# Narrow score products, and expert results weighted in the tile and added by DMA into the output

## The reference, cut to what matters

```python
# layer 0: shifted windows of 64 tokens, 8 heads of 8 channels
qn, kn = q / |q|, k / |k|
attn = einsum('whnd,whmd->whnm', qn, kn) * scale + bias[idx] + mask
out = einsum('whnm,whmd->whnd', softmax(attn), v) @ Wo.T + bo
...
# last layer: 8 experts of width 682, the two best of each token
probs = softmax(flat @ router_w.T)
top_p, top_i = top_k(probs, 2);  top_p = top_p / (sum(top_p) + 1e-9)
h = silu(w1[e] @ x) * (w3[e] @ x);  y[e] = w2[e] @ h
out[n] = t[n] + sum over the two e of top_p * y[e][n]      # t: the residual
```

## Time and profile before

| | |
|---|---|
| median of 3 runs | 1230.27 us (1229.73 to 1235.08) |
| the profiled execution | 1225.98 us, its span 1224.1 us |
| TensorE busy | 957.1 us (78%) |
| VectorE, ScalarE, POOL busy | 814.1, 697.4, 645.7 us |
| moved by DMA | 39.37 MB |

### The profile page before, as it was taken

The page is one execution under the profiler, slowest core; times in us unless marked ns, Lnnn a source line. Parts: engine busy times, 40 slices in busy tenths (PEclk is TensorE's granted clock), DMA queues, the critical chain, the costliest instruction groups (busy, mean ns, idle before and its releaser), DMA issues.

```text
span 1224.1 us, 21611 instructions
## 1 busy us (share of the span) xinstructions
PE 957.1 (78%) x6752; PEld 575.7 (47%) x6752; DVE 814.1 (67%) x1680; ACT 697.4 (57%) x1287; POOL 645.7 (53%) x723
## 2 busy tenths in 40 slices
PE   5869999969997886678686555523999999999960
PEld 3435555534457452334353333311666666666640
DVE  7976666668848335667575444551877787787757
ACT  1815555544462557678564343212888888888850
POOL 3925555516778002003226555564677777777775
PEclk9969999979997997799898787655999999999985
DMA  5000000010023000001100000011011111111105
GB/s 202 1 2 1 1 2 1 2 65 1 1 80 104 0 1 1 1 2 29 48 7 22 20 20 20 19 44 40 26 35 31 34 33 32 35 30 36 30 24 204
DMA packets 24321, 39.37 MB, mean 32 GB/s; under 512 B 6212, under 2 KB 14168, under 8 KB 23960
## 3 DMA queue, kind: packets, MB, share of 16 engines
q1 hardware_dynamic: 15128, 28.62, 7.3%
q0 software_dynamic: 9088, 9.39, 2.4%
HBM read 24.52 MB, written 13.47 MB: 31 GB/s over the span
## 4 chain that ended last, share of the span: by engine, by line
PE 36%; POOL 18%; DVE 18%; issue 15%; ACT 8%; another core or an unknown queue 3%; SPq 1%; DMA 1%; POOLq 0%; DVEq 0%; ACTq 0%
POOL results L709 11%; POOL stage L721 7%; PE bank L1732 5%; PE bank L1743 2%; PE bank L1734 2%; PE bank L1808 2%; PE bank L1982 2%; PE bank L1757 2%; PE bank L1938 1%; PE bank L1961 1%; DVE T L807 1%; PE bank L1821 1%; PE bank L1856 1%; PE bank L1760 1%
## 5 line engine op out<-in xcount | busy, mean ns | idle before, releaser
L2175 PE MATMUL bank<-stage,big 128*114 128x512 f16 x936 | 243.2, 382 | 6.4 <-issue 3.1
L1339 DVE TENSOR_TENSOR T<-bank,T 114x512 f32<-114x512 f32 x234 | 161.5, 690 | 99.7 <-ACT T L1655 83.3
L686 POOL DMA_INDIRECT slots<-T,index x128 | 124.3, 971 | 121.0 <-DVE index L1250 84.5
L709 POOL DMA_INDIRECT results<-stage,small x156 | 153.1, 981 | 37.8 <-issue 37.8
L1655 ACT ACTIVATE T<-bank 114x512 f32<-114x512 f32 x234 | 139.7, 597 | 48.0 <-PE bank L2175 44.4
L2155 PEld LDWEIGHTS bank<-l2w,stage 114*128 114x128 f16 x1872 | 121.0, 98 | 56.2 <-issue 17.5
L1638 ACT ACTIVATE stage<-T 114x512 f16<-114x512 f32 x234 | 146.1, 625 | 0.3 <-DVE T L1339 0.3
L2155 PE MATMUL bank<-l2w,stage 114*128 x1872 | 143.6, 219 | 2.4 <-DVE stage L1349 1.4
L2175 PEld LDWEIGHTS bank<-stage,big 128*114 x936 | 107.9, 131 | 52.2 <-issue 14.6
L721 POOL TENSOR_TENSOR stage<-T,stage 114x512 f16<-114x512 f32 x78 | 89.9, 1153 | 55.7 <-ACT stage L1638 46.8
L1349 DVE TENSOR_TENSOR stage<-T,stage 114x512 f16<-114x512 f32 x156 | 106.4, 682 | 0.0
(11 more groups left out here) (386 smaller groups left out, 2007.9 us busy)
## 6 DMA issues: line engine op xcount, KB each, us to landing
stage<-slots SPq DMA_DIRECT2D x39, 130.0 KB
stage<-in_w1l SPq DMA_DIRECT2D x8, 342.0 KB
stage<-in_w3l SPq DMA_DIRECT2D x8, 342.0 KB
results<-stage,small POOLq DMA_INDIRECT x156
T<-in_xw SPq DMA_DIRECT2D x4, 512.0 KB, 6.0
X<-in_xi SPq DMA_DIRECT2D x1, 2048.0 KB, 14.6
slots<-T,index POOLq DMA_INDIRECT x128
A<-results SPq DMA_DIRECT2D x4, 512.0 KB, 6.7
```

Source lines behind the costliest of these rows:

```text
L686: pool.indirect_dma_start(slots_d, bass.IndirectOffsetOnAxis(ap=index[:, k, n:n + 1], axis=0), rows5[:, n * RW:(n + 1) * RW], None).then_i ...
L709: pool.indirect_dma_start(results_d, bass.IndirectOffsetOnAxis(ap=IDS[t % 4][:, i:i + 1], axis=0), Y5[t % 2][:, i, :], None).then_inc(S(f" ...
L1339: nc.vector.tensor_tensor(H5[q], bank[3 + q][0:HB, :], S5[q], ALU.mult).then_inc(S("hid5"), 1)
L2175: mm = nc.tensor.matmul(bank[q + 3 * (v // 2)][0:HB, :], big16[:, bass.ds(e * (4 * HID3) + (v * HID3 + k * HB), HB)], XT[s], start=(v % 2 ...
```

## The change

In the attention, the queries are no longer staged: the product takes them as 32-row slices of `T1`, and `KX` holds the keys under a mask for 4 slots (128x256). The bias goes first, in four f16 products of 256 columns into two banks, and four f32 products of 32 rows by 64 output rows by 256 columns are added to it. VectorE reads both banks in one instruction. The transposes have one bank (4) instead of two, the sums one (7), the projection gets bank 6; some steps of the groups come one step earlier, and the nine pieces added to the images are split over two steps.

In the last layer, the gate of a row travels with it (`RW` = 2C + 4). POOL copies it out of the tile beside the row number, VectorE multiplies the result by it, and the indirect DMA adds the row to the output, which already holds the residual: SyncE stores that ahead of the expert loop. The output has 512 more rows for results of empty slots. A tile's scatters wait until those of the tile before have landed. The read-back, the mixing and the stores at the end go.

```diff
-RW = 2 * C + 2
+RW = 2 * C + 4
+GATE = C + 1
...
-        QB = [stage[:, s * 128:(s + 1) * 128] for s in range(2)]
-        KX = [stage[:, 512 + s * 512:1024 + s * 512] for s in range(2)]
+        KX = [stage[:, 512 + s * 256:768 + s * 256] for s in range(2)]
...
+        out_rows = out_d.rearrange("q (n c) -> (q n) c", c=C)
...
+        gate5 = T2X[:, :].rearrange("p (n v) -> p n v", v=RW // 2)[:, :, GATE]
...
-            sp.wait_ge(*when("zeros5", 2))
-            empty = zeros5.bitcast(F16).rearrange("p (e v) -> p e v", e=E)
-            sp.dma_start(slots_d[E * CAP:E * CAP + EMPTY * SLOTS, :].rearrange("(t p i) v -> p t (i v)", p=P, i=SUB),
-                         empty[:, 0:EMPTY, :]).then_inc(S("slots_empty"), 16)
+            sp.wait_ge(*when("zeros5", 3))
+            empty = zeros5.bitcast(U32)
+            for i in range(EMPTY):
+                sp.dma_start(slots_d[E * CAP + i * SLOTS:E * CAP + (i + 1) * SLOTS, :]
+                             .rearrange("(p i) v -> p (i v)", i=SUB), empty).then_inc(S("slots_empty"), 16)
+            sp.dma_start(out_rows[2 * P * TILES:2 * P * TILES + SLOTS, :].rearrange("(p i) c -> p (i c)", i=SUB),
+                         zeros_out).then_inc(S("stored"), 16)
+            for c in range(NCH):
+                sp.wait_ge(*chunk("xtok", c))
+                sp.dma_start(out_d[0:P, c * CHUNK:(c + 1) * CHUNK], ch(T4, c)).then_inc(S("stored"), 16)
...
-            back = results_d[0:2 * P * 2 * TILES, :].rearrange("(k p n) c -> k p n c", k=2, p=P)
-            for i in range(4):
-                ns = slice(16 * i, 16 * i + 16)
-                for k in range(2):
-                    sp.dma_start(G5[k][:, ns, :], back[k][:, ns, :]).then_inc(S(f"back_{i}"), 16)
-            for c in range(NCH):
-                if c in (1, 3, 5):
-                    sp.wait_ge(*when("mixed5_pool", c // 2 + 1))
-                else:
-                    sp.wait_ge(*when("mixed5", {0: 1, 2: 2, 4: 3, 6: 4, 7: 5}[c]))
-                sp.dma_start(out_d[:, c * CHUNK:(c + 1) * CHUNK], ch(T4, c)).then_inc(S("stored"), 16)
-            sp.wait_ge(*when("stored", 16 * NCH))
...
-                nc.gpsimd.tensor_tensor(QB[s].rearrange("p (h q) -> p h q", h=2),
-                                        T1[:, bass.ds(n * WT, WT)].unsqueeze(1).broadcast_to([P, 2, WT]),
-                                        vec("half0", 2).unsqueeze(2).broadcast_to([P, 2, WT]),
+                nc.gpsimd.tensor_tensor(KX[s].rearrange("p (h k) -> p h k", h=HP),
+                                        T2[:, bass.ds(n * WT, WT)].unsqueeze(1).broadcast_to([P, HP, WT]),
+                                        slot_mask.unsqueeze(2).broadcast_to([P, HP, WT]),
                                         ALU.mult).then_inc(S("l0_staged"), 1)
-                nc.gpsimd.tensor_tensor(KX[s].rearrange("p (h k) -> p h k", h=HEADS),
-                                        T2[:, bass.ds(n * WT, WT)].unsqueeze(1).broadcast_to([P, HEADS, WT]),
-                                        hmask.unsqueeze(2).broadcast_to([P, HEADS, WT]),
-                                        ALU.mult).then_inc(S("l0_staged"), 1)
...
                     pool.wait_ge(*when(f"sent_0_{q}", 16 * 4 * (c + 1)))
-                    nc.gpsimd.tensor_copy(dest5[:, ns], later5[:, ns]).then_inc(S("dest5_later"), 1)
-                    pool.wait_ge(*when("dest5_later", 2 * c + q + 1))
+                    nc.gpsimd.tensor_copy(gate5[:, ns], gates5[:, 1, ns]).then_inc(S("gate5_later"), 1)
+                    pool.wait_ge(*when("gate5_later", 2 * c + q + 1))
                 for n in range(8 * c + 4 * q, 8 * c + 4 * q + 4):
                     pool.indirect_dma_start(
                         slots_d, bass.IndirectOffsetOnAxis(ap=index[:, k, n:n + 1], axis=0),
-                        rows5[:, n * RW:(n + 1) * RW], None).then_inc(S(f"sent_{k}_{q}"), 16)
-
-            pool.wait_ge(*when("dest5", 2))
+                        rows5u[:, n * (RW // 2):(n + 1) * (RW // 2)], None).then_inc(S(f"sent_{k}_{q}"), 16)
+
             for c in range(NCH):
                 pool.wait_ge(*chunk("rows5_low", c))
+                pool.wait_ge(*chunk("gate5", c))
...
+                nc.gpsimd.tensor_copy(GATES[t % 4], XS[t % 2].bitcast(F32)[:, :, GATE]).then_inc(S("ids5"), 1)
 
             def results5(t, subs):
-                pool.wait_ge(*when("y5", t + 1))
-                pool.wait_ge(*when("ids5", t + 1))
+                pool.wait_ge(*when("gated5", t + 1))
+                pool.wait_ge(*when("ids5", 2 * (t + 1)))
+                if t >= 1:
+                    pool.wait_ge(*when(f"resulted_{(t - 1) % 2}", 16 * SUB * ((t - 1) // 2 + 1)))
+                else:
+                    pool.wait_ge(*when("stored", 16 * (NCH + 1)))
                 for i in subs:
                     pool.indirect_dma_start(
-                        results_d, bass.IndirectOffsetOnAxis(ap=IDS[t % 4][:, i:i + 1], axis=0),
-                        Y5[t % 2][:, i, :], None).then_inc(S(f"resulted_{t % 2}"), 16)
+                        out_rows, bass.IndirectOffsetOnAxis(ap=IDS[t % 4][:, i:i + 1], axis=0),
+                        Y5[t % 2][:, i, :], None, compute_op=ALU.add).then_inc(S(f"resulted_{t % 2}"), 16)
...
-            for c in (1, 3, 5):
-                pool.wait_ge(*when(f"back_{c // 2}", 32))
-                ns = slice(8 * c, 8 * c + 8)
...
-                sc = SC[s].rearrange("p (h k) -> p h k", h=HEADS)
-                biased = bank[s][:, :].rearrange("p (h k) -> p h k", h=HEADS)
+                sc = SC[s].rearrange("p (g h k) -> p g h k", g=2, h=HP)
+                most = rowmax[s].rearrange("p (g h) -> p g h", g=2)
+                biased = banks[:, 2 * s * CHUNK:(2 * s + 2) * CHUNK].rearrange("p (g h k) -> p g h k", g=2, k=WT)[:, :, 0:HP, :]
...
-                nc.vector.tensor_tensor(sc, biased, rowmax[s].unsqueeze(2).broadcast_to([P, HEADS, WT]),
+                nc.vector.tensor_tensor(sc, biased, most.unsqueeze(3).broadcast_to([P, 2, HP, WT]),
                                         ALU.subtract).then_inc(S("l0_shifted"), 1)
...
+            def add_images(c, part):
...
+                for (wy, iy, r, nr), (wx, ix, q, nq) in pieces[5 * part:5 * part + 5]:
...
-                if k % GROUP == 3 and k >= 7 and k // GROUP - 1 < GROUPS:
+                if k % GROUP == 2 and k >= 6 and k // GROUP - 1 < GROUPS:
                     divide_group(k // GROUP - 1)
+                if k % 8 in (3, 4) and k >= 11:
...
+                nc.vector.tensor_copy(gate5[:, 8 * c:8 * c + 8], ga).then_inc(S4("gate5"), 1)
...
+                    gates_of(k - 3)
                     index5(k - 3)
-                    gates_of(k - 3)
...
+                dve.wait_ge(*when("y5", t + 1))
+                dve.wait_ge(*when("ids5", 2 * (t + 1)))
+                nc.vector.tensor_tensor(Y5[s], Y5[s], GATES[t % 4].unsqueeze(2).broadcast_to([P, SUB, C]), ALU.mult) \
+                    .then_inc(S("gated5"), 1)
...
-            for i, c in enumerate((0, 2, 4, 6, 7)):
-                dve.wait_ge(*when(f"back_{c // 2}", 32))
...
-                nc.scalar.activation(PT[n % 2], bank[2 + n % 2][:, :], ACT.Copy).then_inc(S("l0_pt"), 1)
+                nc.scalar.activation(PT[n % 2], bank[4][:, :], ACT.Copy).then_inc(S("l0_pt"), 1)
 
             def invert_sums(m):
                 act.wait_ge(*when("l0_pv", GROUP * (m + 1)))
                 if m >= 2:
                     act.wait_ge(*when("l0_out", m - 1))
-                nc.scalar.activation(RS[m % 2], bank[6 + m % 2][:, :], ACT.Ln).then_inc(S("l0_lnsum"), 1)
+                nc.scalar.activation(RS[m % 2], bank[7][:, :], ACT.Ln).then_inc(S("l0_lnsum"), 1)
...
-                if k % GROUP == 2 and k >= 6:
+                if k % GROUP == 1 and k >= 5:
...
-                pe.wait_ge(*when("l0_staged", (n + 1) * 2))
                 if n >= 2:
                     pe.wait_ge(*when("l0_shifted", n - 1))
-                nc.tensor.matmul(bank[s][:, :], QB[s], KX[s], start=True, stop=False)
-                for v in range(2):
-                    mm = nc.tensor.matmul(bank[s][:, :], ident16[:, 0:128], BM16[:, n % NWIN, v, :], start=False, stop=(v == 1))
+                for g in range(2):
+                    for v in range(2):
+                        nc.tensor.matmul(bank[2 * s + g][:, 0:HP * WT], ident16[:, 0:128],
+                                         BM16[:, n % NWIN, v, g * HP * WT:(g + 1) * HP * WT], start=(v == 0), stop=False,
+                                         skip_group_check=True)
+                pe.wait_ge(*when("l0_staged", n + 1))
+                for g in range(2):
+                    for h in range(2):
+                        r = 64 * h + 32 * g
+                        mm = nc.tensor.matmul(bank[2 * s + g][64 * h:64 * h + 64, 0:HP * WT],
+                                              T1[r:r + 32, n * WT:(n + 1) * WT], KX[s][r:r + 32, :],
```

(32 more changed lines are left out.)

93 lines of the change are left out of this document (36 added, 57 removed).

## The result

The changed kernel takes 1306.72 us (median of 4 runs, 1304.51 to 1309.73) where the kernel before takes 1230.0 (4 runs): ratio 1.0606, interval [1.0583, 1.0629]. It is slower by 77 us. The forecast was 1204 us. The profiled execution took 1309.73 us with a span of 1307.6.

A forecast was written before the change was run, and what follows sets the result against it. No engine is full for long: TensorE and the chain balanced in the attention, POOL near its limit in the loop. -29.0 + 3.9 + 1.7 - 3 = -26.4 from 1230.3 gave 1204 us, range 1186 to 1240.

The forecast's parts named there:

- Term 1: End of the kernel: read-back, mixing and stores leave the path, -31.8 us.
- Term 2: Expert loop: adding scatters wait for the previous tile's landing, taken as 3.1 us; cost 0 in the loop, +1.9 at the end.
- Term 3: Expert loop: POOL generates an adding scatter in 0.97 us as before, at most twice that.
- rival B: Expert loop: generating a scatter takes longer; no gain from a 1.19 us record, about 1346 us at double; chance 0.18.
- rival A: Expert loop: the landing, at 4.07 us, sets POOL's round; 1234 us; chance 0.18.
- Term 4: Expert loop: POOL's copy of the gates costs 0.1 us a tile, +3.9; VectorE's multiplication is hidden, price 0.
- Term 5: Routing stage: gates computed ahead of the indices delay POOL's scatters once, at the stage's end, +1.7 us.
- Term 6: Attention: score products take 0.43 us for 0.96, but the one transposes bank keeps 2.50 a pair; -3 at projections.

The follow-up runs named there:

- low_moved: The changed kernel with a tile's two subtractions moved from GpSimd to VectorE; 1221.6 us against 1183.18 for the kernel before, ratio 1.0326.
- no_add: The changed kernel with plain scatters in place of adding ones, the wait for the landing kept; 1210.7 us, ratio 0.9823 to the kernel before.
- add_free: The kernel before with adding scatters into its results rows and no wait for a landing; 1300.9 us, ratio 1.0547.
- last_only: The changed kernel with layer 0 as before, so the last layer's part of the change alone; 1305.5 us, ratio 1.0567 to the kernel before.
- attn_only: The kernel before with layer 0's attention part of the change alone; 1235.32 us against 1232.58, ratio 1.0021.
- two_turned: The kernel before with layer 0's part of the change and two transposes banks in turn; 1176.33 us against 1183.18, ratio 0.9944.
- gated_mix: The kernel before with gates weighted in the tile, plain scatters, no landing wait, two VectorE additions a chunk at the end; 1183.25 us against 1183.18, ratio 0.9995.

## Why the prediction was wrong

*Term 1, the end goes (-31.8): right.* From the last scatter to the end of the span 34.0 us became 5.5. The text expected "some 3 us"; an adding landing that ends a program takes more.

*Term 2, the wait for the landing: too short, and the second step that failed.* It took 3.1 us for the landing, between 2.17 and 4.07, and 0.1 for the wait: 3.2 from the last scatter of a tile to the first of the next. The runs show 3.81 to 4.12 in nearly all tiles. The landing itself was sized well, 3.2 in low_moved. What was too short is the 0.1: between a landing and GpSimd's next scatter pass some 0.8 us, adding or not. The 2.17 of the earlier trace rows ran to SyncE, which hid that; on POOL, no_add shows 2.95 for a plain scatter. At the end the wait cost 2.5 us (3.81 less a plain spacing of 1.27) in place of 1.9.

*Term 3, the generation of a scatter: this is the step that failed first and most.* "I take 0.97, the row it is nearest to: the number of rows and bytes is the same." Rows and bytes were the same, and the record is 1.56 alone and 1.64 in the median, with spacings of 1.88 to 2.13 in place of 1.27 to 1.30. The two bounds, 0.97 and 1.94, held it. Put into the prediction's own sum, the round of GpSimd was 5.1 us from the first scatter to the fourth, 3.1 for the landing and 0.1: 8.3, inside the 8.53 of a tile. In the tile shown above it is 6.93 (1077.23 to 1084.16) and 4.12: 11.05. Of the 2.75 us too many, 1.83 are generation, three spacings at 0.6 more each, and 0.92 are the wait: two thirds and one third, as add_free has it.

The rule of the text for rival B gives for a record of 1.64: 1204 + 39 x (4 x 0.67 - 0.2) = 1301, near the measured 1306.7, but by luck: it leaves out the longer wait, and it counts four scatters a round where three spacings lie between the first and the fourth. As a check that no large term is missing: 1232.6 + 68.3 of add_free + 33 - 28.5 for the end = 1305.4, against 1305.5 of last_only, from whose period the 33 are taken. Rival B, at 0.18, was the one to come true, with rival A on top. The two share one cause, the adding form, and so they came together; the text priced each alone.

*Term 4, the gates' copy and multiplication (+3.9): no more than that.* no_add has both and the wait for the landing, at 8.81 us a tile against 8.74: 2.6 us for all three. What the copy costs on a GpSimd that has no idle time left, no run separates from the landing.

*Term 5, gates ahead of the indices (+1.7): right in kind, perhaps small.* Putting them back took the ratio from 0.9995 to 0.9965, 3.7 us, with intervals that just overlap, on different chips.

*Term 6, the attention (-3, all else given to the one bank): right in mechanism.* In the kernel after, 32 of the 64 groups of transposes are released by ScalarE's copy, as here:
```profile
231.48 0.63 PE L1733 MATMUL bank<-mats,stage 128*128 128x128 f32 x4 [0.45 <-ACT stage L1392]
...
232.04 0.43 PE L1749 MATMUL bank<-stage,big 128*32 128x128 f32 x8
232.28 0.40 PE L1752 MATMUL bank<-stage,small 128*32 128x128 f32 x8
...
232.62 0.61 PE L1715 MATMUL bank<-big,ident 128*128 128x256 f16 x4
...
233.16 0.66 PE L1722 MATMUL bank<-stage,T 32*64 32x256 f32 x8
233.81 0.63 PE L1733 MATMUL bank<-mats,stage 128*128 128x128 f32 x4
```
From bias to products are 0.54 us, from products to transposes 0.65, each with its change of tiling; the text had 0.54 and 0.54. Less the 0.11 of the change of tiling the four products take 0.54, where the text had 0.43 and one after the other would be 1.7: they overlap, if not wholly. Two pairs take 5.11 us (VectorE's maximum at 228.77 and, two pairs on, at 233.88), forecast 5.00. The -3 at the projections did not come; attn_only lost 2.7, by a mean of 2.64 us a pair against 2.60.

Without the adding form the forecast would have stood: its sum was -26.4, and no_add measured -22. The attention, -3 in the sum and +2.7 measured, more than makes the difference.

## What to carry to other kernels

Before putting a sum into a scatter, ask which engine generates it, and price that engine's spacing, not the transfer: here the bytes stayed, and GpSimd paid 0.6 to 0.8 us more for each of 156 scatters. An engine whose round, with its waits counted in, leaves 0.2 us a tile to spare is the bound for anything more that is given to it, even if its share of busy time reads 72%. Price a wait by what the waiting engine does next, not by what another engine sees: here 0.8 us more. And where two unknown costs hang on the same unknown operation, they are one rival with one chance and a joint price, not two.

## What was not expected of the hardware

The kernel before took 1232.6 us on one chip and 1183.2 on another. The difference lies in the routing stage, whose code is the same in attn_only (first chip) and two_turned (second). The line of the cast of indices in both:
```profile
L1251 DVE CAST index<-small x16: 170/170/172, 637.2 to 816.8; 128x8 uint32<-128x8 f32 x16
```
```profile
L1251 DVE CAST index<-small x16: 170/171/398, 625.1 to 742.8; 128x8 uint32<-128x8 f32 x16
```
The chunks follow each other in 25.7 us on the first and in 16.8 on the second. In attn_only VectorE stands for up to 9.4 us ahead of the small cast of destinations (L1236), six times and 47.6 us in all, released by nothing that the profile shows in five of them; in two_turned it never does. The two chips kept their times, 1226 to 1237 us in 34 executions of the kernel before and 1179 to 1185 in 19. The cause stays open.

A subtraction on GpSimd also stretches one on VectorE. In the tile shown above VectorE's subtraction takes 1.76 us beside it. In low_moved, with as many adding scatters and no subtraction on GpSimd, no instance of VectorE's own takes more than 0.75:
```profile
L1336 DVE TENSOR_TENSOR stage<-T,stage x234: 674/680/751, 819.7 to 1193.3; 114x512 f16<-114x512 f32 x117
```
The Trainium skill says as much ("SBUF — State Buffer", Who interferes with whom): a VectorE instruction with both inputs in SBUF contends with a GpSimd instruction that reads SBUF. The trace of the changed kernel bears it out: of its 156 subtractions on VectorE (L1340), 71 overlap in time with one of GpSimd's and take 1.0 to 2.6 us, 1.8 in the mean, and the other 85 take 0.67 to 0.69.

The adding scatter is not needed for it. At the end of the kernel before, both engines work on f32 operands in SBUF, with no adding scatter anywhere:
```profile
1203.80 1.49 POOL L739 TENSOR_TENSOR A<-A,small 128x512 f32<-128x512 f32 x1
1204.31 1.52 DVE L1365 TENSOR_TENSOR X<-X,small 128x512 f32<-128x512 f32 x1
```
VectorE takes 1.41 to 1.75 us for such an instruction beside GpSimd, twelve times, and 0.68 to 0.69 once GpSimd is done (and 0.69 at 1197.46, where VectorE began first); in gated_mix, with VectorE alone at the end, all sixteen take 0.68 to 0.69. In the expert loop of the kernel before and of no_add the two subtractions meet only once in 156, which is why VectorE's mean is 0.698 us in no_add (the one that met took 1.56). The longer spacings of the adding form shift them onto each other.
